# An eighth embedding table picked by matrix products, transposes one group ahead of their use, and the first table through POOL's queue

## The reference

```python
e = jnp.stack([tbl_0[ids[:, 0]], ..., tbl_25[ids[:, 25]]], axis=1)       # 512 x 26 x 128
sd = jnp.einsum('bfd,bd->bf', e, dense)
ss = jnp.einsum('bfd,bgd->bfg', e, e)
z = jnp.concatenate([dense, sd, ss[:, iu, ju]], axis=1)                  # iu, ju: pairs f < g
h = jnp.concatenate([z, dense], axis=1)
h = jnp.maximum(h @ W_top1 + b_top1, 0.0)                                # 512 wide
h = jnp.maximum(h @ W_top2 + b_top2, 0.0)                                # 256 wide
y = h @ W_top3                                                           # 1 wide
```

## Time and profile before

| | |
|---|---|
| median of 3 runs | 119.66 us (117.87 to 120.6) |
| profiled execution | 118.84 us |
| its span, first to last instruction | 116.9 us |
| PE busy | 104.5 us (89%) |
| PE weight loads | 90.7 us (78%), beside the products |
| DVE, ACT, POOL busy | 63.5, 58.5, 75.7 us |
| mean granted clock of PE | 0.985 |

### The profile page before, as it was taken

How to read it: one execution, slowest core, us unless ns; L and a number is a source line. 1 busy time by engine, 2 the same in 40 slices (tenths; PEclk the granted TensorE clock), 3 DMA queues, 4 the chain that set the end, 5 groups by cost and what they waited for, 6 DMA issues and landing times.

```text
span 116.9 us, 1946 instructions
## 1 busy us (share of the span) xinstructions
PE 104.5 (89%) x696; PEld 90.7 (78%) x696; DVE 63.5 (54%) x140; ACT 58.5 (50%) x133; POOL 75.7 (65%) x88
## 2 busy tenths in 40 slices
PE   0679999999999688999999999978989997899991
PEld 0366676686868475999998998877979996799981
DVE  4779959997999990356746135225220343350030
ACT  4299549939976991255477235535212414340200
POOL 3777777677677767767767767767777775070000
PEclk9999999999999999999999999999999999999599
DMA  2997617362869822212233233112223112011000
GB/s 45 276 275 188 208 52 227 70 203 72 247 201 258 317 83 53 59 45 60 61 72 93 70 78 88 51 45 65 61 68 101 48 45 67 6 25 25 0 0 1
DMA packets 5709, 11.71 MB, mean 100 GB/s; under 512 B 2600, under 2 KB 3070, under 8 KB 5701
## 3 DMA queue, kind: packets, MB, share of 16 engines
q1 hardware_dynamic: 3141, 6.55, 18.9%
q0 software_dynamic: 2560, 5.05, 17.0%
HBM read 10.86 MB, written 0.00 MB: 93 GB/s over the span
## 4 chain that ended last, share of the span: by engine, by line
PE 79%; SPq 6%; DMA 5%; issue 3%; DVE 2%; ACT 2%
PE ps_gram L351 27%; PE ps_gram L410 19%; PE ps_h_bank L438 11%; SPq L275 5%; DMA dense<-in_r_dense_features 4%; PE ps_dve L387 3%; PE ps_h_bank L466 3%; PE ps_h_bank L423 3%; PE ps_act L387 3%; PE ps_gram L342 2%; DMA dots<-sums_even 2%; PE ps_dve L451 2%; PE ps_h_bank L478 1%; PE ps_h_bank L342 1%; PE ps_h_bank L469 1%
## 5 line engine op out<-in xcount | busy, mean ns | idle before, releaser
L323 POOL DMA_INDIRECT rows<-in_cold,cold_rows x72 | 68.8, 955 | 21.9 <-issue 21.3
L410 PE MATMUL ps_gram<-vecs 128*122 128x108 f32 x256 | 30.3, 271 | 2.3 <-ACT vecs L737 1.4
L410 PEld LDWEIGHTS ps_gram<-vecs 128*122 128x122 f32 x256 | 28.6, 187 | 3.5 <-ACT vecs L737 2.5
L351 PE MATMUL ps_gram<-one_hot,table_hi 125*128 125x512 f32 x58 | 24.7, 447 | 1.3 <-issue 1.3
L602 DVE TENSOR_TENSOR one_hot<-ps_gram,row_id 125x1024 fp32r<-125x1024 f32 (+1 forms) x22 | 25.0, 1138 | 0.7 <-PE ps_h_bank L342 0.7
L351 PE MATMUL ps_gram<-one_hot,table_lo 125*128 125x512 f32 x58 | 23.5, 426 | 0.0
L351 PEld LDWEIGHTS ps_gram<-one_hot,table_hi 125*128 125x128 f32 x58 | 11.7, 210 | 5.8 <-issue 3.0
L351 PEld LDWEIGHTS ps_gram<-one_hot,table_lo 125*128 125x128 f32 x58 | 12.0, 207 | 2.7
L438 PE MATMUL ps_h_bank<-dots,w_dots 128*128 128x128 f32 x96 | 13.2, 301 | 0.2 <-DMA dots<-sums_even 0.2
L612 DVE TENSOR_TENSOR table_lo<-table,table_hi 125x256 fp32r<-125x256 f32 x29 | 11.7, 412 | 2.9 <-ACT table_hi L757 2.8
L438 PEld LDWEIGHTS ps_h_bank<-dots,w_dots 128*128 128x128 f32 x96 | 12.7, 215 | 0.4 <-issue 0.4
(11 more groups left out here) (63 smaller groups left out, 96.2 us busy)
## 6 DMA issues: line engine op xcount, KB each, us to landing
table<-in_tbl SPq DMA_DIRECT2D x6, 448.0 KB
rows<-in_cold,cold_rows POOLq DMA_INDIRECT x72, 2.5
w_dots<-in_w_dots SPq DMA_DIRECT2D x1, 768.0 KB, 5.6
table<-in_tbl SPq DMA_DIRECT2D x1, 560.0 KB
w_dense<-in_w_dense SPq DMA_DIRECT2D x1, 512.0 KB, 3.7
w<-in_W_top SPq DMA_DIRECT2D x1, 512.0 KB, 8.2
table<-in_tbl SPq DMA_DIRECT2D x6, 52.0 KB
dense<-in_r_dense_features SPq DMA_DIRECT2D x1, 256.0 KB, 4.2
```

The source lines that it names most:

```text
L323: pool.indirect_dma_start(out=rows[:, t % ROW_SETS, n, :], out_offset=None, in_=ins["cold"], in_offset=bass.IndirectOffsetOnAxis(ap=(cold_ ...
L351: return pe.matmul(ps_pick[:, i % 2, :], part[0:KP, (STEP_AT[i] + k) % PART_STEPS, :], one_hot[0:KP, (STEP_AT[i] + k) % HOT_STEPS, :], sta ...
L410: last = pe.matmul(ps_gram[0:TAKEN, b0 + (g - g0) // PER_BANK, c0:c0 + COLS], vecs[:, t % 2, p0:p0 + QUADS, :].rearrange("d p f -> d (p f) ...
```

## The change

Table 3 joins `HOT`, which has eight tables now, two of them of ten steps (2 and 3) and no longer at the end. There are 68 steps for 58, 18 gathers a tile for 19, and 18 transposes. The first group has two gathers for three. The large part of the first table (112 of 125 partitions) is issued by POOL, as its first instruction. The transposes of tile 0 stand behind the last two picks instead of between the picks, and from then on a group of transposes stands further ahead of the dot products that use it. Layers 1 and 2 of tile 1 move ahead of the last dot products of tile 2. A new semaphore `s_pick_placed` lets the first dot products start before ACT has copied `early`. The orders of DVE and ACT follow.

```diff
-HOT = [5, 6, 7, 16, 19, 24, 2]
+HOT = [5, 6, 2, 7, 16, 3, 19, 24]
...
-KS_ACT = [[4, 5, 6] if i in (1, 2, NHOT - 1) else [4, 5] for i in range(NHOT)]
+KS_ACT = [[4, 5, 6] if i in (1, 3, 5, 7) else [4, 5] for i in range(NHOT)]
...
-EXTRA_WIDTHS = [w for w in (1, 2, 4) if (len(COLD) - MAIN) & w]
-assert EXTRA_WIDTHS[0] == 1
+EXTRA_WIDTHS = [1, 1]
...
-                sp.dma_start(table[0:KP_A, i % TABLE_RING, 0:KTS[i]], whole[0:KP_A]).then_inc(s_table[i], 16)
+
+                if i >= 1:
+                    sp.dma_start(table[0:KP_A, i % TABLE_RING, 0:KTS[i]], whole[0:KP_A]).then_inc(s_table[i], 16)
                 sp.dma_start(table[KP_A:KP, i % TABLE_RING, 0:KTS[i]], whole[KP_A:KP]).then_inc(s_table[i], 16)
...
+            pool.dma_start(table[0:KP_A, 0, 0:KTS[0]], ins[f"tbl_{HOT[0]}"].rearrange("(p k) d -> p k d", k=KTS[0])[0:KP_A]
+                           ).then_inc(s_table_0_pool, 16)
             nc.gpsimd.memset(ident[:, :], 0.0).then_inc(s_zero, 1)
...
                     if t < DIRECT:
-                        pe.wait_ge(s_pick_read, NHOT)
+                        pe.wait_ge(s_pick_placed, NHOT)
...
+                if (t, part) == (0, 1):
+
+                    pe.wait_ge(s_pick_read, NHOT)
...
-            pick(0)
-            pick(1)
+            for i in range(NHOT - 1):
+                pick(i)
             transposes(0, 0)
-            pick(2)
             transposes(0, 1)
-            pick(3)
+            pick(NHOT - 1)
             transposes(0, 2)
...
             gram(2, 2)
             transposes(2, 5)
+            layer_1(1)
+            transposes(2, 6)
             gram(2, 3, 0)
-            transposes(2, 6)
+            layer_2(1)
             gram(2, 3, 1)
-            layer_1(1)
+            layer_3(1)
             transposes(3, 0)
-            layer_2(1)
-            layer_3(1)
             transposes(3, 1)
             layer_1_dense(2)
             gram(3, 0)
+            transposes(3, 2)
             layer_1(2)
-            transposes(3, 2)
+            gram(3, 1)
+            transposes(3, 3)
             layer_2(2)
-            gram(3, 1)
+            gram(3, 2)
             layer_3(2)
-            transposes(3, 3)
-            gram(3, 2)
             transposes(3, 4)
             transposes(3, 5)
             gram(3, 3, 0)
...
             read_sums(3, 0)
+            read_transposed(3, 2)
             relu_1(2)
-            read_transposed(3, 2)
+            read_sums(3, 1)
             relu_2(2)
-            read_sums(3, 1)
+            read_sums(3, 2)
             read_y(2)
             read_transposed(3, 4)
-            read_sums(3, 2)
+            read_sums(3, 3, 0)
             read_transposed(3, 6)
-            read_sums(3, 3, 0)
             read_sums(3, 3, 1)
```

More of the change, by code:

```diff
@@ L168, in build @@
         s_picked = sem("s_picked")
+        s_pick_placed = sem("s_pick_placed")
         s_pick_read = sem("s_pick_read")
@@ L513, in _ @@
             gram(0, 0)
+            transposes(0, 4)
+            gram(0, 1)
+            transposes(0, 5)
+            gram(0, 2)
+            transposes(0, 6)
+            gram(0, 3, 0)
+            transposes(1, 0)
             transposes(1, 1)
-            gram(0, 1)
+            gram(0, 3, 1)
             transposes(1, 2)
-            gram(0, 2)
-            gram(0, 3, 0)
-            gram(0, 3, 1)
+            gram(1, 0)
             transposes(1, 3)
-            gram(1, 0)
+            gram(1, 1)
             transposes(1, 4)
-            gram(1, 1)
+            gram(1, 2)
             transposes(1, 5)
             transposes(1, 6)
-            gram(1, 2)
+            layer_1_dense(0)
             gram(1, 3, 0)
+            transposes(2, 0)
+            transposes(2, 1)
             gram(1, 3, 1)
-            layer_1_dense(0)
-            transposes(2, 0)
             layer_1(0)
-            transposes(2, 1)
+            transposes(2, 2)
             layer_2(0)
@@ L535, in _ @@
             layer_3(0)
-            transposes(2, 2)
+            transposes(2, 3)
+            gram(2, 1)
             layer_1_dense(1)
-            gram(2, 1)
-            transposes(2, 3)
             transposes(2, 4)
@@ L638, in _ @@
                                           ).then_inc(s_dense_read, 1)
-            read_transposed(0, 4)
-            read_transposed(0, 6)
-            read_transposed(1, 0)
+            read_transposed(0, 0)
+            read_transposed(0, 2)
             def read_sums(t, part, piece=None):
@@ L668, in _ @@
             read_sums(0, 0)
+            read_transposed(0, 4)
             read_sums(0, 1)
+            read_sums(0, 2)
+            read_transposed(0, 6)
+            read_sums(0, 3, 0)
+            read_transposed(1, 0)
+            read_sums(0, 3, 1)
             read_transposed(1, 2)
-            read_sums(0, 2)
-            read_sums(0, 3, 0)
-            read_sums(0, 3, 1)
             dve.wait_ge(s_w1_dense, 16)
@@ L679, in _ @@
             read_sums(1, 0)
+            read_sums(1, 1)
             read_transposed(1, 4)
-            read_sums(1, 1)
+            read_sums(1, 2)
             read_transposed(1, 6)
-            read_sums(1, 2)
             read_sums(1, 3, 0)
+            read_transposed(2, 0)
             read_sums(1, 3, 1)
-            read_transposed(2, 0)
             relu_1(0)
+            read_transposed(2, 2)
             relu_2(0)
@@ L751, in round_table @@
             def round_table(i):
-                act.wait_ge(s_table[i], 32)
+                act.wait_ge(s_table[i], 32 if i >= 1 else 16)
+                if i == 0:
+                    act.wait_ge(s_table_0_pool, 16)
                 before = picked_before(STEP_AT[i] + KTS[i] - 1, PART_STEPS)
@@ L791, in _ @@
             read_picked(NHOT - 2)
-            read_transposed(0, 5)
+            read_transposed(0, 1)
             read_picked(NHOT - 1)
+            read_transposed(0, 3)
             def read_sums(t, part, piece=None):
@@ L815, in _ @@
             read_sums(0, 0)
-            read_transposed(1, 1)
             read_sums(0, 1)
+            read_transposed(0, 5)
             read_sums(0, 2)
             read_sums(0, 3, 0)
+            read_transposed(1, 1)
             read_sums(0, 3, 1)
+            read_sums(1, 0)
             read_transposed(1, 3)
-            read_sums(1, 0)
             read_sums(1, 1)
-            read_transposed(1, 5)
             place_early(2)
             read_sums(1, 2)
+            read_transposed(1, 5)
             read_sums(1, 3, 0)
+            read_transposed(2, 1)
             read_sums(1, 3, 1)
             relu_1(0)
-            read_transposed(2, 1)
             relu_2(0)
             read_sums(2, 0)
+            read_transposed(2, 3)
             place_early(3)
             read_sums(2, 1)
-            read_transposed(2, 3)
             read_sums(2, 2)
             read_transposed(2, 5)
+            relu_1(1)
             read_sums(2, 3, 0)
+            relu_2(1)
             read_sums(2, 3, 1)
-            relu_1(1)
-            relu_2(1)
             read_transposed(3, 1)
```

28 lines of the change are left out of this document (7 added, 21 removed).

## The result

The changed kernel takes 125.2 us (median of 4 runs, 124.74 to 126.45), the kernel before 118.96 (4 runs, 117.87 to 120.6). The ratio is 1.065, with a 95% interval of 1.053 to 1.077: slower, clear of noise. The profiled execution took 124.74 us with a span of 122.8, 5.9 above the span before.

What follows compares the result with a forecast made beforehand. PE was taken to bound the kernel, busy 104.5 of 116.9 us, with POOL close behind. 5.5 - 0.4 - 0.8 - 0.3 - 0.5 - 3.3 + 4.9 + 1.6 = +6.7 on 118.84 gave 125.5 us, range 121 to 128.

Steps and rivals of the forecast that it cites:

- The new wait: Before layer_1(2): PE waits for tile 2's strips, 9.2 us of transfers against 4.3 of work, +4.9 us.
- The clock behind it: After the strip wait: PE's clock falls once to half, +1.6 us, between 0 and 3.2.
- Rival 1: At the strip wait: PE waits but its clock stays at full, 123.9 us; chance 0.24.
- The eighth table: Pick stage on PE: ten more steps cost +5.5 us, four transposes fewer give -0.4; fewer gathers gain nothing by themselves.
- The pick stage: Table picks: PE's 1.30 us wait before the last table goes, DVE waits add 0.5; together -0.8 us.
- the start: Kernel start: first table's large part on POOL lets `dense` be issued one issue earlier, -0.3 us, between -0.9 and +0.5.
- the first wait: Before the first dot products: PE's wait of 0.48 us goes, covered by eight transposes, -0.5 us.
- rival 4: Pick stage: DVE uses up its lead and sets the pace, about +3 us, 128.5; chance 0.06.
- The transposes ahead: Behind the picks: six of seven PE waits go, one stays, two small ones are new; net -3.3 us.
- Rival 3: Kernel start: PE reaches full rate sooner, near 116.5 us, only together with rival 2; chance 0.07.
- rival 2: Before layer_1(2): no strip wait to speak of, and no clock fall, 119.0 us, no change; chance 0.13.
- the signs named ahead: Expected traces: 4 to 5 us idle before layer_1(2), half clock, later strips, lost 1.30 us, POOL's last gather 4 us earlier.

Runs made afterwards that it cites:

- a1: The changed kernel with layers 1 and 2 of tile 1 put back behind gram(2, 3, 1): 117.82 us, ratio 1.007 to the kernel before.
- b1: The kernel before with only layers 1 and 2 of tile 1 (and transposes(2, 6)) moved ahead, seven tables: 122.8 us, ratio 1.057.
- a6: The changed kernel with four of tile 2's nine strips issued by ACT, five left on SP: 121.27 us.
- b2: The kernel before with the eighth table and new table order alone, old transposes, layers and queues: 122.95 us against 117.9.
- a4: The kernel of a1 with seven tables, table 3 gathered again, other small tables in the new order: 120.48 us, ratio 1.033.
- a3b: The changed kernel with the whole first table on SP's queue, without POOL's issue: 125.07 us.
- a5: The kernel of a1 with tile 2's layers moved behind gram(3, 1) and gram(3, 2), tile 3's transposes further ahead: 118.15 us, ratio 1.017.
- a0: The changed kernel measured again, unaltered, beside a3b on the same chip: 125.1 us.

## Why the prediction was right

I had forecast 125.5 us; 125.2 came. The mechanism is the one forecast: the wait for tile 2's strips and the fall of the clock behind it make 6.8 us in the profiled execution (4.7 and 2.1), where the sum had 6.5. That the whole came within 0.3 us is partly luck, since single terms of the rest were off by more. Step by step:

- **The new wait, +4.9.** Measured 4.57 of idle, 4.7 with the 0.16 by which the end of a product is modelled too late. The strips landed 9.0 us behind the end of gram(2, 3, 1) against the 9.2 of the forecast, on a cover of 4.3. a1 and b1 show that this edit alone makes most of the loss, a6 that the issues in a row make the wait long.
- **The clock behind it, +1.6.** It fell, and cost 2.1 (5.02 for 2.94): the price was taken from a fall with PE at work, too low by 0.5. Rival 1, the wait without the fall, is out for this wait in all ten executions of the changed kernel (mean clock 0.945 to 0.959). For a shorter wait it was right in a6's profile, with 2.45 us of idle, and wrong in b1's, with 1.85.
- **The eighth table, +5.5 and -0.4.** b2: 5.05 together by the medians, 4.3 to 6.4 at like mean clock. What failed is a side remark, that POOL's four gathers less gain nothing by themselves. In the old order that is so. In the new order the seven-table kernel a4 loses 4.4 us in one wait for rows; the gathers are one part of that, PE's earlier arrival the other.
- **The pick stage -0.8, the start -0.3, the first wait -0.5.** Together with the table and eight transposes fewer ahead of them (0.9) they put the first dot products at 47.25 + 5.5 - 1.6 - 0.9, 50.3 us. They came at 49.3, but with an early rise of PE's rate, which the kernel before did not have in its profile. That was luck. With a late rise, as there, they came at 51.0 and 50.9 (a3b, a5), 0.6 to 0.7 later than forecast. One term that was off is the pick stage: PE waited 1.16 and 0.32 us for DVE's one-hots (+1.5 for my +0.5), as DVE is at work without a break here, which is rival 4's condition. The other is the start: its term is 0 (a0 against a3b). `dense` was issued at 1.94 instead of 2.39 but took 5.0 us to land instead of 4.17, so PE's first transposes stand at 7.11 against 6.69; and ACT's rounding began at 6.07 against 5.71, since POOL's first issue came only at 1.27 and took 4.72 us to land.
- **The transposes ahead, -3.3.** Six waits went as said, and the last two rows of PE's timeline are the two that I had left standing or new (0.63, 0.43); transposes(1, 0) waits 0.32. From a1 and b2, each against the kernel before, the whole rest of the change is worth 4.0 to 5.4 us, around the 4.9 of my four terms. That it is exactly this term is argued; no run had the transposes alone, and two of the six waits stood where the layers of tile 1 moved and are back in a1, by 0.55 and 0.21 us.
- **The tail.** From gram(3, 2) to the last product the changed kernel took 17.0 us against 16.0 before. Of the 1.0, layer 3 of tile 2 (0.4) only changed sides, and the waits are 0.65 us longer, where the sum had 0.5.

Rival 3 had its condition too, the sooner full rate, but without rival 2 it could not make the kernel faster. Of the signs named ahead, the idle stretch, its releaser, the clock, the lost 1.30 us and the later strips (5.0 us later, where I had said 6) are all there. POOL's last gather was not: it came at 97.20 against 97.47, not 4 us earlier.

## What to carry to other kernels

When work is moved ahead of a step, look at what leaves that step by a slow side path and who waits at its far end: the moved work may have been the only cover of that path. Here nine small DMAs in a row took 9 us from the last dot product to the first use, and the order before hid them with 0.2 us to spare. And a wait on PE can cost more than its length, by bringing the clock down: 4.6 us of idle cost 2.1 more, 1.85 us cost 1.6 more in one profile, and 2.45 us nothing more in another. An engine with slack can lose it when another engine comes to its output sooner: weigh a part of a change in the order in which it will stand, not in the old one. And before a difference of 1 or 2 us is put down to an edit, compare executions with the same falls of the clock and the same rise at the start: here each of the two moves the time by about 1.5 us within one kernel.

## What the runs showed of the hardware

- POOL's gathers are uneven in the pick stage of most of these kernels. The kernel before has 4 of them above 1.1 us up to 50 us, and none above 1.17; the changed kernel has 15, up to 1.50, and b2, a1 and a4 have 14, 12 and 12. The line of the gathers has 1018 ns on average against 955. So 72 gathers ended only 0.3 us earlier than 76. a4, with the seven tables of the kernel before in another order, has its 12 as well, so the set of gathers isn't the reason; nor is the place of the transposes, since b2 has the old one. Gathers of 1.3 us and more are in every profile with the new order of the tables, and in neither of the two with the old one (the kernel before and b1, none above 1.17). What in it slows them is open.
- Two gaps of 1.85 us in b1's profile brought the granted clock to 0.50, one of 2.45 us in a6's did not. In the changed kernel the clock fell inside the gap of 4.57 us, in b1 only when PE was back at work: in the windows of 1 us it was still 1.00 where PE took up work again (at 85 and at 92 us), 0.93 and 0.84 in the next, and 0.50 behind them.
- PE ran at half its rate from the first product until 10 to 17 us, with the records showing 1.00 granted in these stretches; the spacing of the products alone shows it (0.43 us for a product of 512 columns, 0.23 behind the rise). The fall near the end comes and goes between executions of one kernel: the mean clock is 1.00 in some and 0.985 in others.
